# Scores over a latent of 64: one FP32 product of 64 rows per head in place of two products of 128 rows over high and low parts

## The reference, cut to what matters

```python
q = (x @ W_q).reshape(B, S, 16, 128).transpose(0, 2, 1, 3)
latent = x @ W_kv_down
kv = (latent @ W_kv_up).reshape(B, S, 16, 128).transpose(0, 2, 1, 3)
scores = jnp.einsum('bhqd,bhkd->bhqk', q, kv) * scale
probs = jax.nn.softmax(scores, axis=-1)
out = jnp.einsum('bhqk,bhkd->bhqd', probs, kv)
return out.transpose(0, 2, 1, 3).reshape(B, S, 2048) @ W_o
```

## Time and profile before

| | |
|---|---|
| median of three executions | 1692.04 us (1689.76 to 1696.74) |
| the profiled execution | span 1695.7 us; of the three times the nearest is 1696.74 us, 1.0 us above it (the page does not say which execution was profiled) |
| PE busy in the whole program | 1441.4 us, 85% |
| POOL, DVE, ACT busy | 773.8, 1075.4, 750.3 us |
| the loop of 128 steps | 1156.9 to 1545 us from the start of the span |
| granted TensorE clock | 0.932 over the span, 1.00 in the loop |

### The profile page before, as it was taken

The page is one execution under the profiler, slowest core; times in us unless marked ns, Lnnn a source line. Parts: engine busy times, 40 slices in busy tenths (PEclk is TensorE's granted clock), DMA queues, the critical chain, the costliest instruction groups (busy, mean ns, idle before and its releaser), DMA issues. The chain is left out here.

```text
span 1695.7 us, 39494 instructions
## 1 busy us (share of the span) xinstructions
PE 1441.4 (85%) x14334; PEld 990.9 (58%) x14334; DVE 1075.4 (63%) x2743; ACT 750.3 (44%) x1786; POOL 773.8 (46%) x741
## 2 busy tenths in 40 slices
PE   6879999448889996888999478877899999998799
PEld 3556656414545554455566356654677777777687
DVE  6852222457876564783222388876998888874888
ACT  5533333254555633553333311125776666752322
POOL 4453332763320000454333466606998888973000
PEclk9989999569999998899999788888999999999899
DMA  8309995631110002514999232200000000000000
GB/s 265 98 14 267 284 266 150 204 96 38 38 38 1 1 1 67 152 40 123 280 296 259 73 87 84 78 4 13 3 16 3 12 7 3 16 3 3 10 19 22
DMA packets 92664, 145.50 MB, mean 86 GB/s; under 512 B 25032, under 2 KB 52528, under 8 KB 92512
## 3 DMA queue, kind: packets, MB, share of 16 engines
q1 hardware_dynamic: 62816, 93.06, 19.1%
q0 software_dynamic: 15360, 37.77, 7.7%
q10 hardware_dynamic: 14336, 12.59, 2.7%
HBM read 122.39 MB, written 18.87 MB: 83 GB/s over the span
## 5 line engine op out<-in xcount | busy, mean ns | idle before, releaser
L2298 POOL TENSOR_TENSOR sb_m_prob<-sb_m_prob,sb_m_rinv 128x512 f32<-128x512 f32 x256 | 260.1, 1041 | 44.6 <-DVE sb_m_rinv L2348 40.8
L1272 POOL DMA_INDIRECT sb_c_rows<-slot_rows,sb_slot x192 | 192.1, 1000 | 102.7 <-issue 51.2
L2228 ACT ACTIVATE sb_m_prob<-m_ps_s,sb_m_nmax 128x512 f32<-128x512 f32 x256 | 173.8, 683 | 125.8 <-DVE sb_m_nmax L2354 125.2
L1106 POOL DMA_INDIRECT e_xn<-xn_rows,sb_table x128 | 117.7, 920 | 209.6 <-PE e_ps_x L1184 197.2
L1255 DVE TENSOR_TENSOR sb_e_h<-sb_e_sg,e_ps_gu 96x176 f32<-96x176 f32 x128 | 42.6, 333 | 256.5 <-ACT sb_e_sg L1231 256.5
L1193 PE MATMUL e_ps_gu<-e_wgu,sb_e_xT 128*96 128x352 f32 x512 | 178.1, 470 | 17.0 <-ACT sb_e_xT L1225 15.6
L2354 DVE TENSOR_REDUCE sb_m_nmax<-m_ps_s 128x1 f32<-128x512 f32 x256 | 163.8, 681 | 28.1 <-PE m_ps_s L2132 25.7
L2362 DVE STREAM_TRANSPOSE sb_m_pT<-sb_m_prob 128x1024 f32<-128x1024 f32 x128 | 157.5, 1232 | 0.0
L2145 PE MATMUL m_ps_v<-sb_m_pT,sb_m_lat_rows 32*64 32x128 f32 x8192 | 136.1, 275 | 4.6 <-issue 3.8
L2131 PE MATMUL m_ps_s<-sb_m_latT_high,sb_m_qa 128*128 128x512 f32 x256 | 125.5, 490 | 16.0 <-ACT sb_m_prob L2228 15.9
L2145 PEld LDWEIGHTS m_ps_v<-sb_m_pT,sb_m_lat_rows 32*64 32x64 f32 x8192 | 120.2, 131 | 27.8 <-issue 27.4
(11 more groups left out here) (280 smaller groups left out, 3076.4 us busy)
## 6 DMA issues: line engine op xcount, KB each, us to landing
e_wgu<-wgu SPq DMA_DIRECT2D x128, 352.0 KB, 4.9
e_wdn<-wdn SPq DMA_DIRECT2D x128, 192.0 KB, 4.7
slot_rows<-sb_e_y ACTq DMA_DIRECT2D x128, 96.0 KB
xn_rows<-e_xn SPq DMA_DIRECT2D x16, 256.0 KB, 2.2
sb_c_rows<-slot_rows,sb_slot POOLq DMA_INDIRECT x192, 2.8
sb_x<-x SPq DMA_DIRECT2D x4, 512.0 KB, 5.4
e_xn<-xn_rows,sb_table POOLq DMA_INDIRECT x128, 5.3
sb_g_zm<-wqT SPq DMA_DIRECT2D x1, 2048.0 KB, 9.1
```

The costliest lines, as they stand in the source:

```text
L1106: pool.indirect_dma_start(x, None, k.xn_rows[:, :], bass.IndirectOffsetOnAxis(ap=k.table[:, e:e + 1], axis=0))\
L1272: pool.indirect_dma_start(rows[u][j][:, :], None, k.slot_rows[:, :], bass.IndirectOffsetOnAxis(ap=k.slot[:, n, j:j + 1], axis=0))\
L2228: act.activation(prob[s % 4][:, hh, :], ps_s[j % 3][:, :], ACT.Exp, bias=nmax[s % 2][:, hh:hh + 1], accum_out=rsum[s % 2][:, hh:hh + 1]).t ...
L2298: pool.tensor_tensor(part, part, rinv[s % 2][:, hh:hh + 1].to_broadcast([P, T]), ALU.mult)\
```

## The change

Latent and queries stay whole FP32. A head's scores are one FP32 product over 64 rows, head A in rows 0 to 63 and head B in rows 64 to 127, each into its own bank. ACT copies the queries once per pair from the bank (`q_copy`) and the latent once per batch (`latT_copy`). POOL and DVE make no low parts. The waits on the parts' semaphores go; scores wait for the copies (`evicted`).

```diff
@@ -2006,7 +2006,6 @@
-    high_ready, q_ready = k.sem("m_high_parts_ready"), k.sem("m_queries_ready")
...
@@ -2046,11 +2043,10 @@
-        latT = [[sb(f"m_latT_{part}{u}", [P, T], F32R) for part in ("high", "low")] for u in range(2)]
+        latT = [sb(f"m_latT{u}", [P, T]) for u in range(2)]
         lat = sb("m_lat", [P, TB, LAT])
         lat_rows = [sb(f"m_lat_rows{u}", [P, TB, TB, LAT]) for u in range(2)]
-        qa = [sb(f"m_qa{u}", [P, 2, T], F32R) for u in range(RING)]
-        q_whole = [sb(f"m_q_whole{u}", [P, T]) for u in range(2)]
+        q = [sb(f"m_q{u}", [P, T]) for u in range(RING)]
...
@@ -2119,17 +2115,17 @@
             def scores(s):
                 pair, t = s // TB, s % TB
-                b, q = s // PER, qa[pair % RING]
+                b = s // PER
                 if t == 0:
-                    pe.wait_ge(q_ready, 2 * (pair + 1))
+                    evicted(pe, ("q", pair))
                     evicted(pe, ("latT", b))
                 cols = slice(t * P, (t + 1) * P)
                 for hh in range(2):
-                    j = 2 * s + hh
+                    j, rows = 2 * s + hh, rows_of(hh)
                     if j >= 3:
                         pe.wait_ge(p_ready, j - 2)
-                    pe.matmul(ps_s[j % 3][:, :], q[:, hh, cols], latT[b % 2][0][:, :], start=True, stop=False)
-                    pe.matmul(ps_s[j % 3][:, :], q[:, hh, cols], latT[b % 2][1][:, :], start=False, stop=True).then_inc(s_ready, 1)
+                    pe.matmul(ps_s[j % 3][:, :], q[pair % RING][rows, cols], latT[b % 2][rows, :], start=True, stop=True)\
+                      .then_inc(s_ready, 1)
...
@@ -2202,22 +2198,15 @@
-            def latT_high(b):
+            def latT_copy(b):
                 full(("latT", b))
-                act.activation(latT[b % 2][0][:, :], bank[:, :], ACT.Copy).then_inc(high_ready, 1)
-
-            def q_high(pair):
+                act.activation(latT[b % 2][:, :], bank[:, :], ACT.Copy).then_inc(bank_free, 1)
+
+            def q_copy(pair):
                 full(("q", pair))
-                if pair >= 2:
-                    act.wait_ge(q_ready, 2 * (pair - 1))
-                act.activation(q_whole[pair % 2][:, :], bank[:, :], ACT.Copy).then_inc(bank_free, 1)
                 if pair >= RING:
                     act.wait_ge(s_ready, 2 * TB * (pair - RING + 1))
-                evicted(act, ("q", pair))
-
-            def q_part(pair, hh):
-                act.activation(qa[pair % RING][rows_of(hh), hh, :], q_whole[pair % 2][rows_of(hh), :], ACT.Copy)\
-                   .then_inc(high_ready, 1)
+                act.activation(q[pair % RING][:, :], bank[:, :], ACT.Copy).then_inc(bank_free, 1)
...
@@ -2281,27 +2263,12 @@
         @block.gpsimd
         def _(pool):
-            def q_low(pair, hh):
-                q = qa[pair % RING]
-                pool.wait_ge(high_ready, high_at[("q", pair)] - 1 + hh)
-                pool.tensor_tensor(q[rows_of(1 - hh), hh, :], q_whole[pair % 2][rows_of(hh), :],
-                                   q[rows_of(hh), hh, :].bitcast(F32), ALU.subtract).then_inc(q_ready, 1)
-                pool.wait_ge(q_ready, 2 * pair + hh + 1)
...
-                for hh in range(2):
-                    key = misc_of(s - 2 - hh)
-                    if key is not None and key[0] == "q":
-                        pool.wait_ge(scaled, 2 * (s + 1))
-                        q_low(key[1], hh)
...
@@ -2321,11 +2288,6 @@
-            def latT_low(b):
-                dve.wait_ge(high_ready, high_at[("latT", b)])
-                dve.tensor_tensor(latT[b % 2][1][:, :], bank[:, :], latT[b % 2][0][:, :].bitcast(F32),
-                                  ALU.subtract).then_inc(bank_free, 1)
```

More of the change, by code:

```diff
@@ L2037, in latent_attention @@
     assert all(n == use_at[key] for n, key in enumerate(uses))
-    halves = [key for key in uses if key[0] in ("latT", "q")]
-    high_at = {key: sum(1 if x[0] == "latT" else 2 for x in halves[:n + 1]) for n, key in enumerate(halves)}
     with ExitStack() as ctx:
@@ L2239, in _ @@
             xT_copy(0, 1)
-            latT_high(0)
+            latT_copy(0)
             for pair in range(2):
-                q_high(pair)
-                for hh in range(2):
-                    q_part(pair, hh)
+                q_copy(pair)
             def miscellany(s):
                 b, e, key = s // PER, s % PER, misc_of(s)
[L2247 to L2253, removed]
+                if key is not None and key[0] == "q":
+                    q_copy(key[1])
                 if b + 1 < B:
@@ L2257, in miscellany @@
                     if e == LATT_AT:
-                        latT_high(b + 1)
+                        latT_copy(b + 1)
                     if e == 10:
@@ L2283, in _ @@
         def _(pool):
-            def q_low(pair, hh):
-                q = qa[pair % RING]
-                pool.wait_ge(high_ready, high_at[("q", pair)] - 1 + hh)
-                pool.tensor_tensor(q[rows_of(1 - hh), hh, :], q_whole[pair % 2][rows_of(hh), :],
-                                   q[rows_of(hh), hh, :].bitcast(F32), ALU.subtract).then_inc(q_ready, 1)
-                pool.wait_ge(q_ready, 2 * pair + hh + 1)
-            for pair in range(2):
-                for hh in range(2):
-                    q_low(pair, hh)
             for s in range(NS):
@@ L2371, in _ @@
                 normalise(0, j)
-            latT_low(0)
             lat_copy(0)
@@ L2375, in evictions @@
                 b, e = s // PER, s % PER
-                if e == LATT_AT and b + 1 < B:
-                    latT_low(b + 1)
                 if e == LATK_AT and b + 1 < B:
```

## The result

| | before | after |
|---|---|---|
| median of the runs, us | 1693.18 (4 runs, 1689.76 to 1696.74) | 1719.16 (4 runs, 1717.19 to 1722.15) |
| profiled execution, time / span, us | its span 1695.7 | 1717.26 / 1715.5 |
| loop, first score of step 0 to first score of step 127, us | 382.1 | 407.0 |
| PE, DVE, ACT, POOL busy, whole span, us | 1441, 1075, 750, 774 | 1470, 1071, 711, 696 |

The changed kernel takes 1.0152 times as long, 95% interval 1.0115 to 1.0190. The forecast was 1716.6 us, in a range of 1693 to 1762. "Slower by over 0.5%" came true. From here on "loop" is the stretch of the table's third line: it leaves out the end of the last step, so that 382.1 us stand where the earlier trace rows have 388.06.

A forecast was written before the change was run, and what follows sets the result against it. PE was taken to bound the kernel, with the score chain where PE has little to do. Terms of -0.75 - 7.7 + 20.4 + 10.3 + 2.3 = +24.6 us on 1692.0 gave 1716.6 us (+1.5%), range 1693 to 1762.

The forecast's parts named there:

- The bound: In the loop, PE is the bound, busy 97.7 of 99.0 us in the second batch; POOL's product is not waited for.
- POOL was the bound after all: Rival: POOL's 79 us in the loop would count, at most down to PE's busy time; given no chance of its own.
- The parts at nothing: In the loop, removing POOL's 79 us of low parts and ACT's 37.5 us of high parts gains nothing.
- Ahead of the loop, -0.75 us: Before the loop, PE's queries no longer wait until DVE's low part gives back the bank: -0.75 us.
- Streaming: Scores of each step: heads side by side take 0.86 us instead of 0.92, 128 x -0.06 = -7.7 us.
- Changes of split: Between row-half scores and whole-array pieces: 102 changes at 0.20 us, +20.4 us, bounds 0 to +30.6.
- Short steps: Steps with only scores: result 0.38 us later, B alone 0.41 longer, 0.79 us for 13 waits, +10.3 us.
- The first steps, +2.3 us: Six bank waits in the first eight steps, without values behind, get only the later result: 6 x 0.38 = +2.3 us.
- The sum: Whole kernel: -0.75 - 7.7 + 20.4 + 10.3 + 2.3 = +24.6 us, giving 1716.6 us; chance 0.60.
- Staggered heads: Rival for the scores: B's first record runs beside A's second, 1.29 us a step, +39 us, 1756 us; chance 0.16.
- Serial heads: Rival for the scores: the heads' products never overlap, 1.72 us a step, 94 us over the forecast, 1810 us; chance 0.07.
- No price for halves: Rival: row halves need no drain, 1696.2 us, or 1683.6 if DVE's lateness also hides short steps; chance 0.17.

The follow-up runs named there:

- The ballast: Changed kernel with 60 ACT copies and 60 POOL subtractions put back on tiles that nobody reads: 1721.16 us.
- the one-pass scores: Changed kernel with latent and queries stored as F32R, each head one pass of 64 rows, low parts left out: 1659.45 us.
- the pair of kernels with and without it: Changed kernel with both heads' scores in the same row half (1790.49 and 1817.93 us), against FP32 products over all 128 rows (1777.69 us).
- the whole-array kernel: Changed kernel with each head's scores as an FP32 product over all 128 rows, summing both heads: 1777.69 us.
- the two kernels with early parts: Kernel before with high and low parts made one step earlier: 1691.03 us with ten pairs' queries split in two pieces, 1691.01 us without.
- split queries: Queries of ten pairs made in two pieces, two steps apart: 1718.75 us on the changed kernel, 1719.78 us on the kernel before.

## Why the prediction was right, by its own steps

**The bound.** PE was read as the bound from its 97.67 of 99.00 us and from DVE's transposes, which never wait. The ballast (nothing) and the one-pass scores (-57.9 us) show both sides of it. "POOL was the bound after all" has fallen.

**The parts at nothing.** Shown for the busy time by the ballast (+1.9 us, all in the first batch) and for the moment at which they come by the parts made one step earlier in the kernel before (-0.3 us of loop).

**Ahead of the loop, -0.75 us.** From the first product of the latent to the first score it was 14.12 us before and is 13.50 now: -0.62.

**Streaming, 128 x -0.06 = -7.7 us.** A step with scores alone took 1.03 us and takes 0.96: -0.07. But the term was counted in the 26 steps of the 13 short chains too, where the chain sets the time; with 102 steps it is -7.1.

**Changes of split, 102 x 0.20 = +20.4 us.** This is the largest term, and its size was worked out from 0.09 and 0.11 us of the earlier trace rows. Measured are 0.196 to 0.200 for each, and 0.195 from the pair of kernels with and without it. The 0.20 was read from values to scores and carried over to other splits; that it holds there as well was assumed, with bounds of 0 to 0.30, and has come out. Groups of four steps bear it out. Steps 84 to 87 hold queries, an output and transposed inputs: five changes, +1.0 - 4 x 0.07 = +0.72; they went from 13.72 to 14.43, +0.71. The Trainium skill ("TensorEngine Tiling (Array Packing)", Key Properties) has a drain at each change of tiling mode. The traces agree: at every such passage the next group's first record starts 0.07 us before the end of the last record, where in the whole-array kernel queries and scores overlap by 0.16. They put a number to it as well, 0.10 us of gap and 0.107 of a load of 128 columns that no longer goes ahead.

**Short steps, 13 x 0.79 = +10.3 us.** The two parts of the term were 0.38 for the later result and 0.41 for B alone. Measured: 2.72 against 2.32 us, +0.40, and B alone 1.05 against 0.66 us, +0.39. The short step and the one behind it went from 1.03 + 3.98 to 0.96 + 4.83: +0.78. Of that only 0.07 is idle time of PE (0.74 against 0.67). Steps 100 to 103, with one such chain and the queries: +0.78 + 0.40 - 2 x 0.07 = +1.04, and they went from 10.82 to 11.84, +1.02.

**The first steps, +2.3 us.** This term came out at about +1.5. For steps 0 to 7 the terms gave -0.5 + 0.8 + 2.3 = +2.6. They went from 19.31 to 19.81 us, but before, four query products fell into 3.4 us at half clock:

```profile
1169.34:1172.75 3.41, 3.41 (x7) 1.67 (x7) 3.41 (x7) 1.93 (x6) 3.25 (x4) 0.50 0.00 0
```

They started over 2.62 us, not 1.31, which leaves 18.0 to 19.8: +1.8 for all that the terms gave +2.6 for. In the changed kernel the same kind of stretch fell into step 8:

```profile
1168.50:1175.10 6.60, 5.01 (x13) 1.56 (x12) 6.11 (x11) 4.30 (x13) 4.80 (x5) 1.00 0.00 1
1175.12:1178.53 3.41, 3.41 (x98) 2.48 (x101) 3.27 (x9) 1.61 (x5) 2.45 (x3) 0.50 0.02 5
```

so that this step took 6.64 us, 1.81 over the others of its kind.

**The sum.** -7.1 + 102 x 0.198 + 13 x 0.78 = +23.2 us of the loop's +24.9 is accounted for. In the 1.7 us left the larger pieces are the first steps (+1.5), the two clock stretches (+1.8 and -1.3), step 36, which took 6.17 us where its kind takes 4.83 (+1.3), and steps 16 and 20, which were already 0.9 and 0.6 us longer than their kind before (-1.5). Step 36 took 5.40 and 5.05 us in the two kernels with early parts as well and 3.98 before. What delays it in the changed kernel is again a stand of PE between two records of the values (0.95 us; the waits from 1259 to 1266 us):

```profile
PE m_ps_v L2141 <- issue: 1.0, 1, 1.0
```

It stands 0.88 to 1.07 us in the same step of the kernels with the ballast, with split queries and with early parts, and not in the kernel before or with serial heads. Its cause is not shown. That the sum comes so near to the loop is thus luck in its last microsecond or two, where a late start, a stand and the stretches of the clock happen to cancel; the three large terms are measured one by one.

**The rivals.** *Staggered heads* would have had B's first record 0.43 us after A's; it is 0.007. The heads' waits between their products don't change that as long as both banks are free. The Trainium skill ("TensorE: Matmul & The Clock Gate", Part 3) has products start strictly in the order of the program. Here B's first record starts 0.007 us after A's first and 0.526 us before A's second. If the two records of a product stand together in the program, which the trace doesn't show, the trace differs from the page here. *Serial heads* are the kernel with both heads in the same rows: 1790 and 1818 us, forecast 1810. *No price for halves* needed a gap under 0.08 us between queries and scores; it is 0.196.

## What to carry to other kernels

Removing work from an engine that is 87% busy gave nothing here, because nobody waited for it. The largest part of the loss, 20.2 of 24.9 us, is how many times the array's split changes. Two products of 64 rows side by side cost 0.96 us against 1.03 for four one-pass products, but every passage between them and whole-array work costs 0.20 us, so row halves don't pay where such products stand singly between others. By these numbers they would in long runs, which no kernel here has. And in a loop where a product waits for a bank that its own result must free, read the chain from start to start (2.32 us, then 2.72): a product that ends 0.4 us later pays twice when the next one also streams alone, and nearly all of that is booked as busy time (0.71 of 0.78 us).

## What had not been expected of the hardware

A wait is not the whole price of a wait. In the split-queries version of the kernel before, TensorE's idle times of about 3 us (22.6 us of them in the loop) stood beside stretches of 3.4 to 6.8 us at a granted clock of 0.5, seven of them in its loop, against one in the loop of the kernel before. The loop's mean clock was 0.96 and it lost 28.7 us against the version whose parts came in time, which has no such stretch: 19.6 us are more waiting, and the other 9.1 are put down to the stretches, without a run that separates them. And the first batch, in which TensorE has the least to do (busy 88.9 of 96.3 us in the changed kernel), has such stretches in eight of the eleven kernels, at other places each time. That is why two loops are compared here by their second and third batches, where a group of four steps repeats to 0.03 us unless a stand as in step 36 or a stretch at half clock falls into it.
